# Selecting carries by one key per node, and scanning node terms with their marks in PSUM, in a four-layer graph network

## The chip, the cores and the metric

The kernel runs on one core of one Trainium2 chip. The metric is the device time of one execution in microseconds. The times of three runs and one further, profiled execution are known.

## The reference

There are 6,250 nodes with 96 features and 200,000 edges sorted by destination. Four residual layers follow each other: a graph attention layer with 4 heads (softmax over the edges that enter a node), two rounds of a segment maximum with edge features, two rounds of a segment mean, and three rounds of a degree-normalised segment sum; after each layer the rows are normalised. What matters here is the attention layer:

```python
h = (x @ W).reshape(N, HEADS, HEAD_DIM)
a_src = jnp.einsum('nhd,hd->nh', h, att_src)
a_dst = jnp.einsum('nhd,hd->nh', h, att_dst)
e = jax.nn.leaky_relu(a_src[src] + a_dst[dst], SLOPE)
m = jax.ops.segment_max(e, dst, num_segments=N)
e = jnp.exp(e - m[dst])
denom = jax.ops.segment_sum(e, dst, num_segments=N)
alpha = e / denom[dst]
out = jax.ops.segment_sum(alpha[:, :, None] * h[src], dst, num_segments=N)
```

## The kernel before

**Layout.** The edges, padded to 128 x 1568, lie so that partition p holds the edges p*T to (p+1)*T-1 (T = 1568), in order of destination. A node's edges are therefore neighbours in one partition, or run over from one partition into the next. A segment sum or maximum is a scan along the free dimension, and what a partition hands to the next one is a "carry".

**The passes.** The first three passes (attention, and the two maxima) gather a row per edge: each pass has 196 slots of 8 edges per partition, a slot has 8 indirect DMAs issued by POOL (L449), and the rows go into a ring of 4 buffers. POOL waits for a buffer until its block has been stored (L486); VectorE combines and scans the block, ScalarE writes it back and stores it. After a pass POOL gathers the last row of each node (L506). The other five passes sum by matmuls over a matrix of counts (L723), which is built during the two maxima passes from "step tables" that VectorE makes in pieces between the slots of the attention pass (`table_piece`, L1325).

**The opening, in order.** POOL gathers runs of destinations (L441), and VectorE gets from them the first edge of every node (`startN`, L1347). From then on:

- POOL gathers slot 0 (L456), writes the attention terms of the nodes to the place of their first edge in DRAM (`ad_starts`, 49 scatters, L460 to L463), gathers slot 1, waits for ARENA to be loaded (`ad_loaded`), gathers one more row of node terms (L467), and goes on with slots 2 to 195.
- SP's queue, in order: it stores the starts, loads the ends (L584), stores the last rows of the nodes (L589), broadcasts them into ROWB (L591), waits for `rowb_used`, broadcasts the starts into ROWB (L593), waits for `rowb_used` again and for the 49 scatters (L595), and loads `ad_starts` into ARENA (L596). ROWB is a part of ARENA.
- VectorE makes the last rows (L1361), the marks `same` (1 where an edge has the same destination as the one before, L1368) and the resets (L1375), and then the selection SEL16, a matrix of 128 partitions by 6,272 nodes: it is 1 where the node's last edge lies in the block of partition p+1 and its first edge before that block. This takes three comparisons (L1379, L1380, L1394), the third on the broadcast starts. PE sums each node's column of it (L845), and VectorE takes the result (L1399).
- Then VectorE waits for the row of L467 (`ad_first`), and spreads the node terms along the edges in a scan for each head (AD is ARENA seen as column by head, so that a head's columns are 4 elements apart): the first 112 columns at L1413, the other 1,456 at L1244, one head in each of the slots 0 to 3 of the attention pass. Those columns are first used in slot 14.

**The attention pass.** At slot u VectorE makes the logits of slot u+1 and the states of slot u (L1450, L1458: the scan whose factors ScalarE has put into PSUM), and then does one piece: pieces 0 to 3 are the scans of L1244, 4 to 24 make the step tables, and after 26 come seven groups of an offset. The order is written out at L1465 to L1472:

```python
if u < 2 * TABLE_ITERS:
    table_piece(u)
elif u < 2 * TABLE_ITERS + NG:
    add_offset(u - 2 * TABLE_ITERS)
```

ScalarE stores each chunk of the tables in a slot fixed by the same count (L937 to L944). ScalarE's order in the opening is the node phase, a square root (L989), and then the attention pass, which begins with a wait for `pass_begun` (L920).

PSUM has psO (2,048 columns of float32), psA, psB and psX. psO holds the products of the node phases, in the attention pass the step tables' sums from piece 11 on, and the products of the carries after it.

Of the kernel before, what the change touches and what calls it, by code (L numbers as in the profile page):

```python
# [80 lines left out]
AD_FIRST = 14 * S  # L81
COLUMNS_SLOT = 12


# [14 lines left out]
def build(nc, x, src, dst, dst_before, src_tiles, dst_tiles, edge_attr, att_W, att_src, att_dst, gat_bias, proj_WT, proj_b, ln_g, ln_b,  # L99
# [7 lines left out]
    def sem(name):  # L107
        return ctx.enter_context(nc.semaphore(name))
# [108 lines left out]
    all_edges = sb("all_edges", [1, 1])  # L217
    bound = sb("bound", [P, 2])
    whole = sb("whole", [P, 1])
# [48 lines left out]
    RUNS = EG[:, 0:2 * GB * RUN].bitcast(I32).rearrange("p (s j r) -> p s j r", s=2, j=GB)  # L268
    BELOW = EG[:, 2 * GB * RUN:3 * GB * RUN].rearrange("p (j r) -> p j r", j=GB)
    SHIFT = SEL16[:, 0:4 * P].bitcast(F32).rearrange("p (a m) -> p a m", a=2)  # L270

# [3 lines left out]
    ETERM = psO[:, :].rearrange("p (s b c) -> p s b c", s=2, b=2)  # L275
    psM = [psA, psB, psX]
    step_sums = [psA[:, 0:CW], psB[:, 0:CW], psX[:, 512:512 + CW]]
    STEP_PS = psO[:, :].rearrange("p (a k) -> p a k", a=4)[:, :, 0:CH]
# [33 lines left out]
    ad_loaded = sem("ad_loaded")  # L312
    ad_first = sem("ad_first")
    gathered = [sem(f"gathered{r}") for r in range(RING)]
    tiles_loaded = sem("tiles_loaded")
# [200 lines left out]
    def _(sp):  # L516
# [75 lines left out]
        sp.wait_ge(rowb_used, 1)  # L592
        sp.dma_start(ROWB, start_row[0:NPAD].partition_broadcast(P)).then_inc(rowb_loaded, 16)  # L593
        sp.wait_ge(rowb_used, 2)
        sp.wait_ge(ad_scattered, 16 * NB)  # L595
# [281 lines left out]
    def _(act):  # L877
# [25 lines left out]
        def attention_pass():  # L903
# [19 lines left out]
            for u in range(SLOTS):  # L923
                if u:
                    act.wait_ge(scanned, u)
                act.wait_ge(exp_in, u + 1)
                nc.scalar.activation(EX[:, u % 2, 0, :, :], EX[:, u % 2, 0, :, :], ACT.Exp).then_inc(scales_made, 1)
                nc.scalar.activation(weights, EX[:, u % 2, 1, :, :], ACT.Exp).then_inc(exp_done, 1)
                if u + 2 < SLOTS:
                    head_resets(u + 2)  # L930
                act.wait_ge(scales_made, u + 1)
                nc.scalar.copy(scales[:, :, 1:K9].rearrange("p (h w) k -> p h w k", w=HW),
                               EX[:, u % 2, 0, :, 1:K9].unsqueeze(2).broadcast_to([P, HEADS, HW, S])).then_inc(scales_ready, 1)
                if u:
                    rows_back(u - 1)
                    store(u - 1)
                c = (u - 2 - COLUMNS_SLOT) // 3  # L937
                if (u - 2 - COLUMNS_SLOT) % 3 == 0 and c in range(CHUNKS):
                    act.wait_ge(stage_ready, c + 1)
                    act.dma_start(step_cols[:, :, c * CH:(c + 1) * CH], STAGE[:, c % 2, :, :]  # L940
                                  ).then_inc(stage_stored[c % 2], 16)
                if u == 2 * TABLE_ITERS + 1:
                    act.wait_ge(step_row_ready, 1)
                    act.dma_start(step_rows, ROW_I[:, 0, :]).then_inc(step_row_stored, 16)  # L944
# [73 lines left out]
        node_phase(ATT)  # L1018
        root(dis[:, :])
        attention_pass()  # L1020
        exp(QT[:, 1, :])
# [66 lines left out]
    def _(dve):  # L1088
# [52 lines left out]
        link(nc.vector.tensor_copy(bound[:, 0:1], bound_i[:, :]))  # L1141
        link(ts(bound[:, 1:2], bound[:, 0:1], float(T), None, ALU.add))

# [98 lines left out]
        def ad_along_rest(h):  # L1242

            link(nc.vector.tensor_tensor_scan(out=AD[:, AD_FIRST:T, h], data0=same[:, AD_FIRST:T], data1=AD[:, AD_FIRST:T, h],  # L1244
                                              initial=AD[:, AD_FIRST - 1, h:h + 1], op0=ALU.mult, op1=ALU.add))
# [114 lines left out]
        dve.wait_ge(ends_back, 16)  # L1360
        link(ts(lastf[:, :], ends[:, :], -1.0, 0.0, ALU.add, ALU.max))  # L1361
        dve.sem_inc(rows_out, 1)
        dve.wait_ge(node_idx, 1)
# [14 lines left out]
        dve.wait_ge(rowb_loaded, 16)  # L1378
        link(ts(SEL16, ROWB, bound[:, 0:1], None, ALU.is_ge))  # L1379
        link(stt(SEL16, ROWB, bound[:, 1:2], SEL16, ALU.is_lt, ALU.mult))  # L1380
        dve.sem_inc(rowb_used, 1)
# [10 lines left out]
        link(ts(wneg[:, :], wrow[:, :], -1.0, BIG, ALU.add, ALU.mult))  # L1392
        dve.wait_ge(rowb_loaded, 32)
        link(stt(SEL16, ROWB, bound[:, 0:1], SEL16, ALU.is_lt, ALU.mult))  # L1394
        dve.sem_inc(rowb_used, 1)
        dve.sem_inc(small_ready, 1)
# [12 lines left out]


        dve.wait_ge(ad_first, 16)
        for h in range(HEADS):
            link(nc.vector.tensor_tensor_scan(out=AD[:, 0:AD_FIRST, h], data0=same[:, 0:AD_FIRST], data1=AD[:, 0:AD_FIRST, h],  # L1413
                                              initial=0.0, op0=ALU.mult, op1=ALU.add))
# [6 lines left out]
        def attention_pass():  # L1421
# [43 lines left out]
            for u in range(SLOTS):  # L1465
                if u + 1 < SLOTS:
                    logits(u + 1)
                states(u)
                if u < 2 * TABLE_ITERS:
                    table_piece(u)  # L1470
                elif u < 2 * TABLE_ITERS + NG:
                    add_offset(u - 2 * TABLE_ITERS)  # L1472

# [380 lines left out]
```

## Time and profile before

| what | us |
|---|---|
| median of 3 runs | 8222.67 |
| lowest and highest | 8220.35, 8223.56 |
| the profiled execution, its time | 8213.33 |
| the profiled execution, its span | 8211.5 |

| engine | busy us | share of the span |
|---|---|---|
| PE (matmul) | 4235.5 | 52% |
| VectorE | 5538.0 | 67% |
| ScalarE | 1494.4 | 18% |
| POOL | 4891.3 | 60% |

A busy share is an average over stages. The span has an opening of about 208 us, three passes of gathers up to about 6570 us, and 1641 us of sums by matmul. The chain of waits follows the end of the span back, at each step to what released it; "issue" is time in which an engine waited for nothing that the profile shows. POOL's DMA instructions are rows of its own with a duration; a row in brackets at the end of a line tells how long the engine was idle before it, and what ended that.

### The profile page before, as it was taken

Reading aid. Unit: us, or ns where it says so; the run is one execution under the profiler, and the core shown is the slowest. Engines: PE = TensorE matmul, PEld = TensorE weight load, DVE = VectorE, ACT = ScalarE, POOL = GpSimd, SP = SyncE. Lnnn points to the kernel's source line nnn. Section 1 sums busy time; section 2 is a strip of 40 time slices with the busy share of each in tenths; the row PEclk is TensorE's granted clock in tenths of the full one; section 3 lists DMA queues with packets and bytes.
Section 4 is the critical chain, followed back from the end, with each engine's and each line's share of the span. In section 5 each row is a group of like instructions: output and inputs, shape, how many; then the busy total and the mean of one; then the engine's idle time right before and its main releaser. Section 6 shows DMA issues by size and latency. Waiting matters only on the chain.

```text
span 8211.5 us, 69615 instructions
## 1 busy us (share of the span) xinstructions
PE 4235.5 (52%) x19184; PEld 2465.7 (30%) x19184; DVE 5538.0 (67%) x13229; ACT 1494.4 (18%) x2140; POOL 4891.3 (60%) x5030
## 2 busy tenths in 40 slices
PE   2100000000155655656555555556565498999999
PEld 1000000000131111111113111111111298999999
DVE  4765555555578888888886888888888775222222
ACT  0222222222231121111111111111211200010000
POOL 6777777777637777777776777777777600000000
PEclk6555555555566565565655555565555599999999
DMA  5333333333224444444443444444444275766767
GB/s 145 86 93 86 85 86 85 86 85 86 66 86 130 129 129 132 131 130 130 129 130 103 129 130 132 130 130 129 130 131 131 80 263 201 267 225 227 268 220 247
DMA packets 642303, 1132.83 MB, mean 138 GB/s; under 512 B 164860, under 2 KB 422287, under 8 KB 641634
## 3 DMA queue, kind: packets, MB, share of 16 engines
q1 hardware_dynamic: 360256, 440.38, 16.7%
q0 software_dynamic: 159184, 251.10, 15.5%
q10 hardware_dynamic: 122578, 438.40, 13.4%
q14 instruction: 210, 1.72, 0.1%
q8 instruction: 75, 1.23, 0.1%
HBM read 716.67 MB, written 412.70 MB: 138 GB/s over the span
## 4 chain that ended last, share of the span: by engine, by line
POOL 57%; PE 20%; issue 18%; DVE 3%; ACT 1%; DMA 1%; DVEq 0%; POOLq 0%; ACTq 0%; SPq 0%
POOL CG L449 55%; PE psB L723 6%; PE psX L723 6%; PE psA L723 6%; PE psO L668 1%; POOL ad_starts L461 1%; POOL EG L506 1%; ACT X L1001 1%; POOL EG L441 0%; PE psX L660 0%; PE psO L783 0%; DVE BUF L1120 0%; DVE EG L1172 0%; PE psO L671 0%; DVE halves L1176 0%
## 5 line engine op out<-in xcount | busy, mean ns | idle before, releaser
L449 POOL DMA_INDIRECT CG<-table,BUF x4704 | 4532.5, 964 | 1564.2 <-issue 1432.1
L695 PE MATMUL psO<-WE,BUF 128*128 128x384 f32 x1568 | 1137.3, 880 | 106.8 <-DMA BUF<-in_edge_attr 99.8
L766 PE MATMUL psA<-ident,F 128*100 128x128 f32 x1 | 0.5, 452 | 1740.0 <-DVEq L1404 1740.0
L475 POOL CAST CG<-EG x35 | 26.9, 769 | 1297.9 <-DVEq L1173 1297.9
L953 ACT COPY psX<-BUF 128x384 f32<-128x384 f32 x392 | 189.0, 482 | 3210.7 <-DVE STG L1531 1618.2
L695 PEld LDWEIGHTS psO<-WE,BUF 128*128 128x128 f32 x1568 | 460.6, 324 | 619.4 <-DMA BUF<-in_edge_attr 371.6
L1429 DVE TENSOR_TENSOR terms<-CG,ARENA 128x32 f32<-128x32 f32 x196 | 45.1, 230 | 792.5 <-DMA CG<-table,BUF 792.0
L1493 DVE TENSOR_SCALAR BUF<-iota,EG 128x392 bf16<-128x392 f16 x1568 | 542.3, 346 | 0.0
L766 PEld LDWEIGHTS psA<-ident,F 128*100 128x100 f32 x1 | 0.2, 158 | 1740.3 <-DVEq L1404 1740.3
L702 PE MATMUL psB<-BUF 128*128 128x392 bf16 x523 | 251.2, 480 | 511.4 <-DVE BUF L1499 511.2
L702 PE MATMUL psA<-BUF 128*128 128x392 bf16 x523 | 252.1, 482 | 506.4 <-DVE BUF L1499 506.4
L723 PE MATMUL psA<-CG,BUF 128*128 128x288 bf16 x4018 | 509.9, 287 | 6.2 <-DMA BUF<-counts 6.2
L723 PE MATMUL psB<-CG,BUF 128*128 128x288 bf16 x4018 | 509.2, 287 | 7.1 <-DMA BUF<-counts 7.1
L702 PE MATMUL psX<-BUF 128*128 128x392 bf16 x522 | 251.4, 482 | 504.6 <-DVE BUF L1499 504.6
L1490 DVE TENSOR_SCALAR BUF<-iota,EG 128x128 bf16<-128x128 f16 x1568 | 496.4, 317 | 20.6 <-DMA EG<-step_rows 20.6
L723 PE MATMUL psX<-CG,BUF 128*128 128x288 bf16 x3969 | 500.8, 286 | 0.6 <-POOL CG L478 0.6
L723 PEld LDWEIGHTS psA<-CG,BUF 128*128 128x128 bf16 x4018 | 495.4, 142 | 9.5 <-POOL CG L478 6.7
L723 PEld LDWEIGHTS psB<-CG,BUF 128*128 128x128 bf16 x4018 | 495.1, 142 | 9.8 <-issue 7.5
L1499 DVE TENSOR_SCALAR BUF<-iota,EG 128x392 bf16<-128x392 f16 x1568 | 495.9, 316 | 0.0
L723 PEld LDWEIGHTS psX<-CG,BUF 128*128 128x128 bf16 x3969 | 488.3, 142 | 1.6 <-POOL CG L478 0.8
L1524 DVE TENSOR_TENSOR XTQ<-CG,psO 128x768 f32<-128x768 f32 x196 | 288.6, 1473 | 216.5 <-DMA CG<-table,BUF 216.3
L1524 DVE TENSOR_TENSOR STG<-CG,psO 128x768 f32<-128x768 f32 x196 | 288.8, 1473 | 207.4 <-DMA CG<-table,BUF 206.8
(279 smaller groups left out, 7912.3 us busy)
## 6 DMA issues: line engine op xcount, KB each, us to landing
BUF<-counts SPq DMA_DIRECT2D x245, 784.0 KB, 5.8
BUF<-counts ACTq DMA_DIRECT2D x245, 784.0 KB, 6.2
counts<-BUF SPq DMA_DIRECT2D x1572, 98.0 KB, 2.4
hist<-CG ACTq DMA_DIRECT2D x392, 384.0 KB, 2.5
hist<-CG ACTq DMA_DIRECT2D x196, 416.0 KB, 2.6
CG<-table,BUF POOLq DMA_INDIRECT x4704
BUF<-in_edge_attr SPq DMA_DIRECT2D x392, 128.0 KB
table<-TB SPq DMA_DIRECT2D x14, 336.0 KB, 2.6
```

The costliest lines, as they stand in the source:

```text
L449: pool.indirect_dma_start(out=rows_in[:, u % RING, k, :], out_offset=None, in_=tab, in_offset=bass.IndirectOffsetOnAxis(ap=SRC[:, u * S + ...
L461: pool.indirect_dma_start(out=ad_starts, out_offset=bass.IndirectOffsetOnAxis(ap=start_i[:, b:b + 1], axis=0), in_=ADN[:, b, :], in_offset ...
L506: pool.indirect_dma_start(out=EG[:, b * width:(b + 1) * width], out_offset=None, in_=rec, in_offset=bass.IndirectOffsetOnAxis(ap=last_i[:, ...
L668: mm = pe.matmul(OUTG[:, k, 0:cols], XT[0:depth, g % 2, k * P:(k + 1) * P], WR[0:depth, f, 0:cols], start=True, stop=f != PROJ)
L695: mm = pe.matmul(ETERM[:, s, a, 0:4 * DIM], EA[:, s, a, :], WE[:, m, :, :].rearrange("k c d -> k (c d)"), start=True, stop=True)
L702: pe.matmul(sums, LO[:, j, 0, :], RHS[:, j, 0, :], start=True, stop=False)
L723: mm = pe.matmul(sums[:, 0:3 * DIM], CNT16[:, B % 3, b:b + NB * (P - 1) + 1:NB], PARTS[:, b, :], start=b == 0, stop=b == NB - 1, skip_grou ...
L953: nc.scalar.copy(reset_cols[:, :, 1:K9], reset[:, u * S:(u + 1) * S].unsqueeze(1).broadcast_to([P, DIM // 2, S])).then_inc(resets_ready, 1)
L1490: ts(LO[:, j, 0, :], iota16[:, 0:P], STEP[:, 2, n:n + 1], None, ALU.is_equal)
L1493: ts(RHS[:, j, 0, :], iota16[:, :], STEP[:, 0, n:n + 1], None, ALU.is_equal)
L1499: ts(RHS[:, j, 1, :], iota16[:, :], STEP[:, 1, n:n + 1], None, ALU.is_equal).then_inc(onehot_ready, 1)
L1524: tt(max_cols[b][:, :, 1:K9].rearrange("p c (a k) -> p c a k", a=2), ROWSW[:, r, :, :].rearrange("p (a k) c -> p c a k", a=2), ETERM[:, s, ...
```

## The change

The last row of a node and its first are turned into block numbers (e // T, by a shift, a multiplication and a shift in integers). The node's key is T times the block of its last row, or 0 where both lie in one block. The key is what SP stores and broadcasts, and a single equality with the partition's bound, T*(p+1), gives SEL16. The second broadcast, the second and third comparison, the second wait of SP and the second bound go. ScalarE copies the marks `same` to PSUM (SAME, in psO) after its square root, and the eight scans of node terms read them there, after a wait for that copy. All pieces of the attention pass begin in slot 4 in place of slot 0, with ScalarE's stores of the tables.

```diff
@@ -80,6 +80,9 @@
 COLUMNS_SLOT = 12
+PIECES_FROM = 4
+SPLIT_BITS, SPLIT_MULT, SPLIT_SHIFT = 5, 2675, 17
+assert all(((e >> SPLIT_BITS) * SPLIT_MULT) >> SPLIT_SHIFT == e // T for e in range(EPAD + 1))
@@ -215,7 +218,7 @@
-    bound = sb("bound", [P, 2])
+    bound = sb("bound", [P, 1])
@@ -267,6 +270,7 @@
+    KEY = EG[0:NB, 3600:3600 + 2 * P].bitcast(I32).rearrange("p (a m) -> p a m", a=2)
@@ -274,6 +278,7 @@
+    SAME = psO[:, 0:T]
@@ -311,6 +316,7 @@
+    same_copied = sem("same_copied")
@@ -590,8 +596,6 @@
         sp.dma_start(ROWB, last_row[0:NPAD].partition_broadcast(P)).then_inc(rowb_loaded, 16)
         sp.wait_ge(rowb_used, 1)
-        sp.dma_start(ROWB, start_row[0:NPAD].partition_broadcast(P)).then_inc(rowb_loaded, 16)
-        sp.wait_ge(rowb_used, 2)
         sp.wait_ge(ad_scattered, 16 * NB)
@@ -934,12 +938,13 @@
-                c = (u - 2 - COLUMNS_SLOT) // 3
-                if (u - 2 - COLUMNS_SLOT) % 3 == 0 and c in range(CHUNKS):
+                piece = u - PIECES_FROM
+                c = (piece - 2 - COLUMNS_SLOT) // 3
+                if (piece - 2 - COLUMNS_SLOT) % 3 == 0 and c in range(CHUNKS):
...
-                if u == 2 * TABLE_ITERS + 1:
+                if piece == 2 * TABLE_ITERS + 1:
@@ -1017,6 +1022,7 @@
         root(dis[:, :])
+        nc.scalar.copy(SAME, same).then_inc(same_copied, 1)
         attention_pass()
@@ -1139,7 +1145,6 @@
-        link(ts(bound[:, 1:2], bound[:, 0:1], float(T), None, ALU.add))
@@ -1241,7 +1246,7 @@
-            link(nc.vector.tensor_tensor_scan(out=AD[:, AD_FIRST:T, h], data0=same[:, AD_FIRST:T], data1=AD[:, AD_FIRST:T, h],
+            link(nc.vector.tensor_tensor_scan(out=AD[:, AD_FIRST:T, h], data0=SAME[:, AD_FIRST:T], data1=AD[:, AD_FIRST:T, h],
@@ -1359,6 +1364,13 @@
         link(ts(lastf[:, :], ends[:, :], -1.0, 0.0, ALU.add, ALU.max))
+        link(nc.vector.tensor_copy(KEY[:, 0, :], starts[:, :]))
+        link(nc.vector.tensor_copy(KEY[:, 1, :], lastf[:, :]))
+        link(ts(KEY, KEY, SPLIT_BITS, None, ALU.logical_shift_right))
+        link(ts(KEY, KEY, float(SPLIT_MULT), None, ALU.mult))
+        link(ts(KEY, KEY, SPLIT_SHIFT, None, ALU.logical_shift_right))
+        link(tt(ends[:, :], KEY[:, 0, :], KEY[:, 1, :], ALU.is_lt))
+        link(stt(lastf[:, :], KEY[:, 1, :], float(T), ends[:, :], ALU.mult, ALU.mult))
         dve.sem_inc(rows_out, 1)
@@ -1376,8 +1388,7 @@
         dve.wait_ge(rowb_loaded, 16)
-        link(ts(SEL16, ROWB, bound[:, 0:1], None, ALU.is_ge))
-        link(stt(SEL16, ROWB, bound[:, 1:2], SEL16, ALU.is_lt, ALU.mult))
+        link(ts(SEL16, ROWB, bound[:, 0:1], None, ALU.is_equal))
         dve.sem_inc(rowb_used, 1)
@@ -1390,9 +1401,6 @@
-        dve.wait_ge(rowb_loaded, 32)
-        link(stt(SEL16, ROWB, bound[:, 0:1], SEL16, ALU.is_lt, ALU.mult))
-        dve.sem_inc(rowb_used, 1)
         dve.sem_inc(small_ready, 1)
@@ -1408,9 +1416,10 @@
+        dve.wait_ge(same_copied, 1)
         dve.wait_ge(ad_first, 16)
         for h in range(HEADS):
-            link(nc.vector.tensor_tensor_scan(out=AD[:, 0:AD_FIRST, h], data0=same[:, 0:AD_FIRST], data1=AD[:, 0:AD_FIRST, h],
+            link(nc.vector.tensor_tensor_scan(out=AD[:, 0:AD_FIRST, h], data0=SAME[:, 0:AD_FIRST], data1=AD[:, 0:AD_FIRST, h],
@@ -1466,10 +1475,11 @@
                 states(u)
-                if u < 2 * TABLE_ITERS:
-                    table_piece(u)
-                elif u < 2 * TABLE_ITERS + NG:
-                    add_offset(u - 2 * TABLE_ITERS)
+                piece = u - PIECES_FROM
+                if 0 <= piece < 2 * TABLE_ITERS:
+                    table_piece(piece)
+                elif 0 <= piece < 2 * TABLE_ITERS + NG:
+                    add_offset(piece - 2 * TABLE_ITERS)
```

## Rows read from the trace of the kernel before

**Rows 1.** The page's chain that ended last, by line.

```profile
POOL CG L449 55%; PE psB L723 6%; PE psX L723 6%; PE psA L723 6%; PE psO L668 1%; POOL ad_starts L461 1%; POOL EG L506 1%; ACT X L1001 1%; POOL EG L441 0%; PE psX L660 0%; PE psO L783 0%; DVE BUF L1120 0%; DVE EG L1172 0%; PE psO L671 0%; DVE halves L1176 0%
```

**Rows 2.** Groups by line, POOL: operation, count, busy us, mean ns, idle us and releasers.

```profile
L449 POOL DMA_INDIRECT CG<-table,BUF x4704 | 4532.5, 964 | 1564.2 <-issue 1432.1 <-DMA table<-TB 131.5 <-DVEq L1238 0.3
...
L461 POOL DMA_INDIRECT ad_starts<-ADN,start_i x49 | 64.3, 1312 | 14.9 <-issue 14.9
```

**Rows 3.** Chain in order of time, 190 to 230 us: start, length, what.

```profile
195.10 10.78 DMA ARENA<-ad_starts
...
206.64 0.94 POOL ARENA L467
```

**Rows 4.** Timeline of POOL, 127 to 171 us: start, length, instruction, idle before.

```profile
130.54 1.70 POOL L461 DMA_INDIRECT ad_starts<-ADN,start_i  x1 [0.31 <-issue]
132.55 0.98 POOL L461 DMA_INDIRECT ad_starts<-ADN,start_i  x1 [0.30 <-issue]
...
141.70 4.21 POOL L461 DMA_INDIRECT ad_starts<-ADN,start_i  x1 [0.30 <-issue]
146.21 6.48 POOL L461 DMA_INDIRECT ad_starts<-ADN,start_i  x1 [0.30 <-issue]
...
163.29 7.48 POOL L461 DMA_INDIRECT ad_starts<-ADN,start_i  x1 [0.30 <-issue]
```

**Rows 5.** Timeline of VectorE, 128 to 211 us.

```profile
128.57 0.42 DVE L1361 TENSOR_SCALAR lastf<-ends 49x128 f32<-49x128 f32 x1 [16.32 <-DMA ends<-start_row]
...
129.60 1.79 DVE L1368 TENSOR_TENSOR BUF<-CG 128x1568 f32<-128x1568 int32 x1
...
141.57 3.48 DVE L1379 TENSOR_SCALAR SEL<-ARENA,bound 128x6272 bf16<-128x6272 f32 x1 [6.73 <-DMA ARENA<-last_row]
145.09 6.75 DVE L1380 SCALAR_TENSOR_TENSOR SEL<-ARENA,bound,SEL 128x6272 bf16<-128x6272 f32 x1
...
163.16 6.75 DVE L1394 SCALAR_TENSOR_TENSOR SEL<-ARENA,bound,SEL 128x6272 bf16<-128x6272 f32 x1 [8.62 <-DMA ARENA<-start_row]
171.62 0.21 DVE L1399 TENSOR_SCALAR cpen<-psB 128x49 f32<-128x49 f32 x1 [1.71 <-PE psB L845]
209.03 1.67 DVE L1413 TENSOR_TENSOR_SCAN ARENA<-BUF,ARENA 128x112 f32<-128x112 f32 x4 [37.20 <-DMA ARENA<-ad_nodes,dst]
```

**Rows 6.** Timeline of VectorE, 216 to 255 us.

```profile
216.23 2.03 DVE L1458 TENSOR_TENSOR_SCAN STG<-psX,STG 128x900 f32<-128x900 f32 x1
218.18 3.23 DVE L1244 TENSOR_TENSOR_SCAN ARENA<-BUF,ARENA 128x1456 f32<-128x1456 f32 x1
...
246.24 0.21 DVE L1429 TENSOR_TENSOR terms<-CG,ARENA 128x32 f32<-128x32 f32 x1 [3.69 <-DMA CG<-table,BUF]
...
251.72 3.23 DVE L1244 TENSOR_TENSOR_SCAN ARENA<-BUF,ARENA 128x1456 f32<-128x1456 f32 x1
```

**Rows 7.** Timeline of POOL, 216 to 256 us.

```profile
216.81 0.94 POOL L449 DMA_INDIRECT CG<-table,BUF  x1 [0.30 <-issue]
...
219.30 2.85 POOL L449 DMA_INDIRECT CG<-table,BUF  x1 [0.30 <-issue]
...
227.46 3.30 POOL L449 DMA_INDIRECT CG<-table,BUF  x1 [0.30 <-issue]
...
239.80 3.50 POOL L449 DMA_INDIRECT CG<-table,BUF  x1 [0.30 <-issue]
...
252.39 3.31 POOL L449 DMA_INDIRECT CG<-table,BUF  x1 [0.30 <-issue]
```

**Rows 8.** Timeline of ScalarE, 153 to 214 us.

```profile
153.22 0.24 ACT L989 ACTIVATE dis<-dis 128x49 f32<-128x49 f32 x1 [75.67 <-DVEq L1387]
211.50 0.34 ACT L908 COPY reset_heads<-BUF 128x32 f32<-128x32 f32 x2 [58.04 <-DVEq L1463]
...
213.52 0.82 ACT L932 COPY psX<-EX 128x800 f32<-128x800 f32 x1
```

**Rows 9.** Timeline of VectorE, 39 to 40 us.

```profile
39.78 0.15 DVE L1142 TENSOR_SCALAR bound<-bound 128x1 f32<-128x1 f32 x1
```

## The prediction

> **What bounds the kernel now.** The chain of waits comes first: POOL's row gathers of L449 hold 55% of the span, more than all matmuls together [rows 1]. The groups by line say how tightly: the 4,704 gathers take 964 ns each, and of the 1,564.2 us that POOL idles before them 1,432.1 us is "issue", 0.30 us ahead of each; the rest is three waits for a node table [rows 2]. There is no idle time before a gather that waits for a stored block or for another engine's result. So through the three edge passes POOL sets the pace, and whatever shortens POOL there shortens the kernel one for one. The opening is POOL's too: 49 scatters at L461, 64.3 us with 14.9 us of issue [rows 2], then the load of the node terms into ARENA, then one gather, then the stream of gathers [rows 3].
>
> The mean of a scatter is 1,312 ns [rows 2], the ordinary one 0.98 us. The timeline shows where the rest is: four take 1.70, 4.21, 6.48 and 7.48 us [rows 4]. Laid beside VectorE's timeline, the last three each fall under one long VectorE instruction and end 0.8 to 0.9 us after it: 4.21 under the selection's first comparison (141.57 to 145.05), 6.48 under the second (L1380, to 151.84), 7.48 under the third (L1394, to 169.91) [rows 4, 5]. The broadcast loads of the selection's rows aren't the cause: the first is under way until the comparison that waits for it begins at 141.57, and the scatter at 132.55 still takes 0.98 [rows 4, 5]. The same is seen at the four long scans of L1244, 3.23 us each: the gather that each catches takes 2.85, 3.30, 3.50 and 3.31 us where 0.94 is ordinary [rows 6, 7]. The scan of L1458, 2.03 us, has one operand in PSUM, and the gather at 216.81, wholly under it, takes 0.94 [rows 6, 7]. So what holds POOL is a VectorE instruction that reads two tensors of SBUF (or that runs at two elements per cycle, as L1379 does: 6,272 in 3.48 us), and not one with one operand in PSUM. POOL is held for about the instruction's length, less the part in which POOL did other things.
>
> **The change, part by part, on POOL's path.**
>
> The two comparisons L1380 and L1394 go, each over 6,272 columns with SEL16 and ROWB read from SBUF. The scatters under them give back 6.48 - 0.98 = 5.50 us and 7.48 - 0.98 = 6.50 us: 12.0 us in all. The comparison that stays (is_equal for is_ge, same shape and types) I keep at 3.48 us and its stall at 4.21 - 0.98 = 3.23 us. Its start moves against POOL's beat of 1.29 us, so the stall may be 2.5 to 3.5; were is_equal to run at one element a cycle, with its single SBUF input it would hold POOL as little as L1458 does, and the 3.23 us would go too. Both ends go into the range.
>
> The scatters end 12.0 us sooner, and so must what follows. The ARENA load starts when the last scatter has landed, at 195.10 [rows 3]. Its other condition is the release of ROWB, on SP's queue ahead of it: now the second release, after 169.91, later the only one, after the comparison that ends at 145.05 today [rows 5]. The keys push that by 2 us, to about 147, against 183 for the last scatter: 36 us of cover. So all 12.0 us arrive at the load and at the first gather behind it. SP also loses one broadcast load of 3.1 MB; it lies beside the scatters and is worth nothing.
>
> The keys add seven VectorE instructions on 49 partitions by 128 or 256 elements. The same 49 by 128 takes 0.42 us in L1361 [rows 5], the nearest row; with 0.03 us between them that is at most 3.2 us, and the like of 0.2 us (a small operation, as L1399 [rows 5]) gives 1.6 at least. I take 2.0. They stand before the store of the last rows, so SP's store, the broadcast load and the comparison all come 2 us later; VectorE is next wanted by POOL's path only at 209.03, after 37.20 us of idleness [rows 5] that become some 37.2 - 12.0 - 2.0 + 6.75 + 6.75 + 8.62 (the wait for the second load, gone) = 45 us. That wait hides the keys; with the cover gone, they would cost their 2.0 us. On POOL they may add little stalls, and they shift the comparison of L1368, which today costs 1.70 - 0.98 = 0.72 us and could cost 0 to 1.5. I take +0.3 for all of that, with -0.9 and +1.6 as ends.
>
> The copy of the marks into PSUM is ScalarE's, 1,568 columns. ScalarE copies 800 columns to PSUM in 0.82 us, so some 1.6 us [rows 8], and twice that would change nothing. It starts behind the root at 153.22, where ScalarE is idle for 58.04 us [rows 8]. The added wait for it stands on VectorE ahead of the four short scans and of everything of the pass, but the copy is done near 155 and those scans begin near 197. Zero.
>
> The scans of node terms now have one operand in PSUM. In length I leave them at 3.23 us: 2.22 ns per column, against 2.03/900 = 2.26 for the scan that reads PSUM already [rows 6]. For POOL they become like L1458: 2.85 + 3.30 + 3.50 + 3.31 - 4 x 0.94 = 9.2 us are given back [rows 7]. The trace has no scan with this step of four elements and a PSUM operand, so the saving has the bounds 0 (it still holds POOL) and 9.2; the nearest row is L1458, also a scan, and I take 9.2. The four short scans of L1413, 1.67 us together [rows 5], get the same operand; of 112 columns each, they slip between POOL's accesses already, and I count nothing.
>
> Moving the pieces to the fifth slot is worth about nothing. In the first slots VectorE is behind, and it catches up sooner; but POOL waits for it in neither case [rows 2]. With the scans, a slot of VectorE is 251.72 - 246.24 + 3.23 = 8.7 us [rows 6], and POOL's is 8 x (0.94 + 0.31) = 10.0, so VectorE keeps 1.3 us to spare where it now has 3.69. The terms scanned in slots four to seven are first read in slot 14. ScalarE's stores of the tables and the offsets move along with the pieces, four slots or 40 us, into a pass of 196 slots. The other short stalls of the pieces go with them unchanged. The instruction of L1142 leaves the opening chain: 0.2 us [rows 9].
>
> The sum: -12.0 - 9.2 - 0.2 + 0.3 = **-21.1 us**. On the profiled execution (span 8211.5, time 8213.33) that is 8192.2. The median of the runs is 8222.67, 9.3 us above that execution; the stalls are of fixed length, so I take the same 21.1 us off it: 8201.6, -0.26%.
>
> On such stalls the Trainium skill says (SBUF — State Buffer, the practical consequences of its port section) that an instruction with two SBUF inputs blocks a GpSimd instruction only on its reads, and infers that descriptor generation needs the write interface alone. By that inference neither the comparisons nor the scans would hold a gather, and the sum would be about zero; the 7.48 us scatter under L1394 speaks against it [rows 4].
>
> **The rivals.** (a) The scans keep holding POOL, because of their length or their stepped output in SBUF, of which the trace has no case with PSUM. For it: only that absence. Against: L1458 and the gathers under it. Then -12.0 alone counts: 8222.67 - 12.0 = 8210.7. Chance 0.08.
>
> (b) VectorE's two-operand instructions don't hold POOL; the long scatters and gathers have another cause that only coincides with them, so the comparisons go and the scans change, and the stalls stay. 8222.7 (plus or minus 1). Against it: each long entry starts under a long VectorE instruction and ends within 0.9 us of its end [rows 4 to 7]. Chance 0.03. The skill's inference above would end here.
>
> (c) Slower. The scans with their stepped SBUF operand and a PSUM operand run far slower than either row, and VectorE becomes the bound in slots four to seven. The first 1.3 us more per scan are free, then the ring of four buffers lends about one slot (10 us, an estimate: a block is stored about 20 us after its gather, its buffer wanted after 30). With x us more per scan the loss is 4(x - 1.3) - 10. It eats the 21.1 us at x = 9.1, that is at scans of 12.3 us, 8.5 ns per column against 2.26 measured. At six times today's length (x = 16.2) it is 8222.7 + 49.6 - 21.1 = 8251. Chance 0.01.
>
> (d) Unforeseen shifts of phase between POOL and VectorE over the three passes, either way by several us; the gathers' mean of 964 against 944 ns is 94 us of such stalls in all [rows 2]. A twentieth of it more or less is 5 us. Chance that this takes the result out of the forecast's own range: 0.04, half of it towards no gain.
>
> **How the numbers follow.** The forecast has 0.84. Its own range: down by 3.2 (the remaining comparison not holding POOL) and 0.9, up by 1.6 and by some 3 of phase and of run scatter (the three runs lie within 3.2 us): 8197 to 8206. To reach rival (a), at 8210.7, the range goes up to 8211: with (a) it holds 0.92 of the cases on paper, and less allowing for what I have not seen. About 0.2%, or 16.4 us, is what a measurement of this kernel can tell from no change. The forecast with its range is beyond it (8206.2 is the border): faster 0.83. Rivals (a) and (b) and half of (d) are within: same 0.14. Slower, (c) and the unforeseen: 0.03.
>
> **What the profile after would show.** No scatter over 5 us, just one of about 4.2 under the equality; scatters' total down from 64.3 to about 52 us; the ARENA load starting near 183 and the first gather behind it near 196; the four scans in slots four to seven at 3.2 to 3.3 us, with the gathers beside them at 0.94; VectorE's idle time ahead of the first scan longer, not shorter. I am wrong if those gathers still take 3.3 us (a), if a scatter of 6 us remains (b), if POOL idles before a gather for a stored block (c), or if all of this is seen and the pass still ends less than 18 us sooner (d).

## The result and the profile after

The changed kernel takes 8200.35 us (median of 9 runs, 8191.73 to 8204.42), the kernel before 8221.36 beside it (9 runs, 8220.16 to 8226.31). The difference is 21.0 us; the ratio is 0.9971 with a 95% interval of 0.9963 to 0.9979. The forecast was 8201.6, 21.1 us below. (A few executions of either kernel in the groups below took hundreds or thousands of microseconds longer; the ratios leave them out.) The profiled execution of the changed kernel took 8202.16 us, its span 8200.2. That is only 11.3 us shorter than the span of before, and why it is so is a finding of its own (last section).

The groups by line of POOL, after (the answer to [rows 2]):

```profile
L455 POOL DMA_INDIRECT CG<-table,BUF x4704 | 4532.3, 963 | 1567.5 <-issue 1432.6 <-DMA table<-TB 134.3 <-DVEq L1243 0.3
...
L467 POOL DMA_INDIRECT ad_starts<-ADN,start_i x49 | 52.0, 1060 | 14.9 <-issue 14.9
```

The scatters took 64.3 us and take 52.0. The waits ahead of the gathers are of the same kinds as before: 1432.6 us of issue, 134.3 us for the three node tables, 0.3 us for VectorE, and none for a stored block. (The row of before has the 0.3 us too; the prediction took it as nothing.)

POOL's timeline from 135 to 147 us, the answer to [rows 4]:

```profile
135.03 1.43 POOL L467 DMA_INDIRECT ad_starts<-ADN,start_i  x1 [0.30 <-issue]
...
145.93 4.04 POOL L467 DMA_INDIRECT ad_starts<-ADN,start_i  x1 [0.30 <-issue]
```

These are the only two scatters above 1.2 us. Where four were long, there is the one that runs into the comparison of destinations (1.43) and the one that runs into the equality (4.04). The timeline of VectorE from 130 to 255 us answers to [rows 5, 6]:

```profile
130.99 0.22 DVE L1367 CAST EG<-starts 49x128 int32<-49x128 f32 x1
...
132.93 0.28 DVE L1373 SCALAR_TENSOR_TENSOR lastf<-EG,ends 49x128 f32<-49x128 int32 x1
...
146.36 3.48 DVE L1391 TENSOR_SCALAR SEL<-ARENA,bound 128x6272 bf16<-128x6272 f32 x1 [7.31 <-DMA ARENA<-last_row]
...
197.25 1.67 DVE L1422 TENSOR_TENSOR_SCAN ARENA<-psO,ARENA 128x112 f32<-128x112 f32 x4 [42.72 <-DMA ARENA<-ad_nodes,dst]
...
242.97 3.23 DVE L1249 TENSOR_TENSOR_SCAN ARENA<-psO,ARENA 128x1456 f32<-128x1456 f32 x1
247.47 0.21 DVE L1438 TENSOR_TENSOR terms<-CG,ARENA 128x32 f32<-128x32 f32 x1 [1.27 <-DMA CG<-table,BUF]
```

The seven instructions of the keys take 2.2 us (130.99 to 133.21). The equality takes 3.48 as the comparison did, the scan with its marks in PSUM 3.23 as the one without. VectorE idles 42.72 us ahead of the short scans, so all that was added there is covered.

POOL's timeline from 194 to 257 us, the answer to [rows 3, 7]: the gather behind the load, and gathers beside two of the long scans.

```profile
194.85 0.95 POOL L473 DMA_INDIRECT ARENA<-ad_nodes,dst  x1 [2.54 <-DMA ARENA<-ad_starts]
...
243.64 0.95 POOL L455 DMA_INDIRECT CG<-table,BUF  x1 [0.31 <-issue]
244.89 0.95 POOL L455 DMA_INDIRECT CG<-table,BUF  x1 [0.30 <-issue]
...
253.65 0.94 POOL L455 DMA_INDIRECT CG<-table,BUF  x1 [0.31 <-issue]
```

The gather at 243.64 lies wholly under the scan of 242.97 to 246.20 and takes 0.95 us; before, such a one took 3.3. The row at 206.64 of before has come to 194.85, 11.8 us sooner. ScalarE's copy to PSUM, in its timeline near 151 us:

```profile
151.53 1.46 ACT L1025 COPY psO<-BUF 128x1568 f32<-128x1568 f32 x1
```

### The profile page after: what moved, and what is told of

Read it like the earlier page. It is cut to its first block, busy times and chain, and to the rows that moved or that the text cites. A ratio compares the mean times of both kernels' runs of the same rounds, so it can differ in the third digit from the quotient of the medians.

```text
span 8200.2 us, 69617 instructions
## 1 busy us (share of the span) xinstructions
PE 4244.0 (52%) x19184; PEld 2467.5 (30%) x19184; DVE 5524.8 (67%) x13233; ACT 1496.4 (18%) x2141; POOL 4879.7 (60%) x5030
## 4 chain that ended last, share of the span: by engine, by line
POOL 57%; PE 20%; issue 19%; DVE 3%; ACT 1%; DMA 1%; DVEq 0%; POOLq 0%; ACTq 0%; SPq 0%
POOL CG L455 55%; PE psX L727 6%; PE psB L727 6%; PE psA L727 6%; PE psO L672 1%; POOL EG L447 1%; POOL EG L512 1%; POOL ad_starts L467 1%; ACT X L1006 1%; PE psX L664 0%; DVE EG L1177 0%; PE psO L787 0%; DVE BUF L1126 0%; PE psO L675 0%; DVE halves L1181 0%
## 5 line engine op out<-in xcount | busy, mean ns | idle before, releaser
L455 POOL DMA_INDIRECT CG<-table,BUF x4704 | 4532.3, 963 | 1567.5 <-issue 1432.6
## 6 DMA issues: line engine op xcount, KB each, us to landing
BUF<-in_edge_attr SPq DMA_DIRECT2D x392, 128.0 KB
```

What stands on the lines that cost most here:

```text
L455: pool.indirect_dma_start(out=rows_in[:, u % RING, k, :], out_offset=None, in_=tab, in_offset=bass.IndirectOffsetOnAxis(ap=SRC[:, u * S + ...
```

## The experiments

Four groups of runs, each with runs of the kernel before on its own chip, and a probe that was executed once, in group 3 (8205.33 us, read for its rows alone). The median of before is 8221.36, 8214.86, 8223.48 and 8211.74 us in the four, so only distances within a group are compared.

| kernel | group | us, median | to before, us | ratio, 95% interval |
|---|---|---|---|---|
| changed | 1 | 8200.35 | -21.0 | 0.9971 (0.9963 to 0.9979) |
| changed, again | 2 | 8189.31 | -25.5 | 0.9971 (0.9958 to 0.9983) |
| scans from SBUF | 2 | 8197.78 | -17.1 | 0.9980 (0.9971 to 0.9989) |
| key alone | 2 | 8199.98 | -14.9 | 0.9982 (0.9973 to 0.9991) |
| scans alone | 2 | 8203.17 | -11.7 | 0.9987 (0.9978 to 0.9997) |
| equality in 16 | 3 | 8196.72 | -26.8 | 0.9970 (0.9958 to 0.9981) |
| all cut short | 3 | 8187.79 | -35.7 | 0.9959 (0.9945 to 0.9973) |
| changed, beside | 3 | 8198.82 | -24.7 | 0.9971 (0.9960 to 0.9981) |
| all cut short, again | 4 | 8176.60 | -35.1 | 0.9954 (0.9940 to 0.9967) |
| changed, third | 4 | 8190.90 | -20.8 | 0.9975 (0.9966 to 0.9984) |

### The changed kernel again

No edit.

> The changed kernel once more, to see what varies by itself. Theory: in the opening and in slots 4 to 7 the same rows as in its first profile (first gather behind the load near 196, no gather over 1.0 us beside the four scans), but an ordinary gather's period that may be anything from 1.248 to 1.251 us, and a time that follows it: 4,704 gathers x 2.4 ns = 11 us between a profile with the one and with the other. Rival: the longer period (1.2509 us against 1.2484 before) is a price of the change itself; then it is seen here again, and never in the kernel before.

Measured: the ordinary gather takes 944 ns here, as in the kernel before, where the first profile of the same changed kernel had 947. The longer period is no price of the change; it comes and goes between executions of one kernel (rows in the last section). The span is 8187.5 us, and the same stretch of the opening is as short as in the first profile.

### Scans from SBUF

```diff
-            ... data0=SAME[:, AD_FIRST:T] ...
+            ... data0=same[:, AD_FIRST:T] ...
-        nc.scalar.copy(SAME, same).then_inc(same_copied, 1)
-        dve.wait_ge(same_copied, 1)
```

and the same for the four short scans.

> The changed kernel, but the eight scans read their marks from SBUF again, and the copy to PSUM is gone; the pieces still begin in the fifth slot. Theory (the second SBUF operand holds POOL): the four gathers beside the long scans take 2.85 to 3.5 us again, 9.2 us in all, and the time is 9 us above the changed kernel: about 8209.5. Rival (the gain of the scans came from their later slot, where VectorE no longer lags): those gathers stay at 0.95 us, and the time is that of the changed kernel, 8200.

Measured: 8.5 us above the changed kernel of its group (8197.78 to 8189.31). Both engines' timelines from 241 to 283 us; the other two scans look the same:

```profile
241.41 3.23 DVE L1248 TENSOR_TENSOR_SCAN ARENA<-BUF,ARENA 128x1456 f32<-128x1456 f32 x1
242.08 3.31 POOL L455 DMA_INDIRECT CG<-table,BUF  x1 [0.30 <-issue]
...
278.52 3.23 DVE L1248 TENSOR_TENSOR_SCAN ARENA<-BUF,ARENA 128x1456 f32<-128x1456 f32 x1
279.19 3.31 POOL L455 DMA_INDIRECT CG<-table,BUF  x1 [0.30 <-issue]
```

In slots 4 to 7 a scan with both operands in SBUF costs POOL 3.31 - 0.94 = 2.37 us, 9.5 in all. The operand does it; the later slot doesn't end the holding. (The 8209.5 of the expectation was counted from group 1; within the group 9 us were expected and 8.5 measured.)

### The key alone

The kernel above with `PIECES_FROM = 0`: of the change, only the key, the equality and the loads and comparisons that went.

> The kernel before with the key and the single equality alone: scans from SBUF, pieces from the first slot. Theory (two comparisons of 6.75 us held POOL for 5.50 and 6.50 us): 12 us below the kernel before, about 8209.5, no scatter over 5 us, and the same as the kernel with scans from SBUF in the fifth slot to within 2 us, since the slot is worth nothing. Rival (the later slot is worth something): 3 us or more above that kernel.

Measured: 14.9 us below before where 12 were expected, 2.2 above the kernel with the scans in the fifth slot. The long gathers beside the scans take 2.85, 3.31, 3.31 and 3.31 us: 9.0 us over the ordinary, against 9.5 in the later slots. The slot is worth nothing by the rows, and 2.2 us of medians (2 were expected at most) is within what executions differ. The scatters are down to 52.5 us.

### The scans alone

The keys' seven instructions go, the second bound comes back, and:

```diff
-        link(ts(SEL16, ROWB, bound[:, 0:1], None, ALU.is_equal))
+        link(ts(SEL16, ROWB, bound[:, 0:1], None, ALU.is_ge))
+        link(stt(SEL16, ROWB, bound[:, 1:2], SEL16, ALU.is_lt, ALU.mult))
+        sp.dma_start(ROWB, start_row[0:NPAD].partition_broadcast(P)).then_inc(rowb_loaded, 16)
+        sp.wait_ge(rowb_used, 2)
+        link(stt(SEL16, ROWB, bound[:, 0:1], SEL16, ALU.is_lt, ALU.mult))
```

> The changed kernel with the three comparisons, the second broadcast load and its wait put back, and the keys taken out: only the scans' part of the change. Theory: 9 us below the kernel before, about 8212, the scatters of 6.5 and 7.5 us back, total of the scatters near 64 us. Were the two parts to share a gain (one hidden by the other), this and the key alone would add up to more or less than the 21.0 us of both together; by the theory they add up.

Measured: 11.7 us below before where 9 were expected. Both engines' timelines from 142 to 173 us:

```profile
142.56 3.96 POOL L467 DMA_INDIRECT ad_starts<-ADN,start_i  x1 [0.30 <-issue]
...
146.42 6.75 DVE L1388 SCALAR_TENSOR_TENSOR SEL<-ARENA,bound,SEL 128x6272 bf16<-128x6272 f32 x1
146.82 7.21 POOL L467 DMA_INDIRECT ad_starts<-ADN,start_i  x1 [0.30 <-issue]
...
164.49 6.75 DVE L1402 SCALAR_TENSOR_TENSOR SEL<-ARENA,bound,SEL 128x6272 bf16<-128x6272 f32 x1 [8.60 <-DMA ARENA<-start_row]
164.63 7.46 POOL L467 DMA_INDIRECT ad_starts<-ADN,start_i  x1 [0.30 <-issue]
```

With the comparisons the two long scatters are back at once; the scatters' total is 65.0 us. The second broadcast load is back too, but it isn't what holds POOL: of the eight scatters from 154.33 us on, most of them in the 8.60 us in which VectorE waits for it, none takes more than 0.99 us.

By the medians of one group the two parts add up: 14.9 + 11.7 = 26.6 us alone, 25.5 together. The rows give less. The last gather of the first pass starts at 2155.07 us with the key alone and at 2159.54 with the scans alone, against 2166.51 before: 11.4 and 7.0 us, 18.4 in sum, where both together have 20.1 (below). So neither part hides the other, but the 3 us by which each median exceeds its expectation are not explained by the edit.

### The probe

```diff
+        for _ in range(3):
+            link(tt(PC, PA, PB, ALU.add))
+        for _ in range(3):
+            link(tt(PC, SAME, PB, ALU.add))
+        for _ in range(2):
+            link(ts(PC, PA, 1.0, None, ALU.mult))
+        for _ in range(2):
+            link(ts(PC, SAME, 1.0, None, ALU.mult))
+        for _ in range(2):
+            link(stt(PC, PA, 1.0, PB, ALU.mult, ALU.add))
         dve.wait_ge(ad_first, 16)
```

PA, PB and PC are unused parts of SBUF of 1,568 columns; two of them are filled with zeros first.

> The changed kernel with a row of VectorE instructions of 1,568 float32 columns each, put under the later scatters, where VectorE has nothing to do (behind the column sums of the selection, ahead of the wait for the node terms): three additions of two SBUF tensors, three of one PSUM and one SBUF tensor, two scalings SBUF to SBUF, two scalings PSUM to SBUF, two multiply-and-adds of two SBUF tensors. They compute nothing that is used. Theory (two SBUF inputs, or the fast mode, hold POOL): each scatter that falls under an addition or multiply-and-add of two SBUF tensors takes 0.5 to 1.7 us more than 0.98, and under a fast scaling (about 1 us) 0.1 to 0.9 more; under the forms with PSUM every scatter takes 0.98, the additions being as long as the others. Rival (length alone holds POOL, or any use of SBUF): the forms with PSUM cost the same as those without. Rival from the page's inference (a tensor_tensor takes only the read interface): the additions of two SBUF tensors cost nothing either, and only the scalings do.

VectorE's timeline from 154 to 175 us, equal instructions merged:

```profile
154.45 5.45 DVE L1424 TENSOR_TENSOR BUF<-BUF 128x1568 f32<-128x1568 f32 x3
159.93 5.44 DVE L1426 TENSOR_TENSOR BUF<-psO,BUF 128x1568 f32<-128x1568 f32 x3
165.41 1.99 DVE L1428 TENSOR_SCALAR BUF<-BUF 128x1568 f32<-128x1568 f32 x2
167.43 3.62 DVE L1430 TENSOR_SCALAR BUF<-psO 128x1568 f32<-128x1568 f32 x2
171.08 3.69 DVE L1432 SCALAR_TENSOR_TENSOR BUF<-BUF 128x1568 f32<-128x1568 f32 x2
```

POOL's timeline over the same stretch:

```profile
154.36 0.98 POOL L467 DMA_INDIRECT ad_starts<-ADN,start_i  x1 [0.30 <-issue]
155.64 1.45 POOL L467 DMA_INDIRECT ad_starts<-ADN,start_i  x1 [0.30 <-issue]
157.40 1.52 POOL L467 DMA_INDIRECT ad_starts<-ADN,start_i  x1 [0.31 <-issue]
159.23 1.52 POOL L467 DMA_INDIRECT ad_starts<-ADN,start_i  x1 [0.30 <-issue]
161.05 0.98 POOL L467 DMA_INDIRECT ad_starts<-ADN,start_i  x1 [0.30 <-issue]
162.34 0.98 POOL L467 DMA_INDIRECT ad_starts<-ADN,start_i  x1 [0.30 <-issue]
163.62 0.98 POOL L467 DMA_INDIRECT ad_starts<-ADN,start_i  x1 [0.30 <-issue]
164.91 1.59 POOL L467 DMA_INDIRECT ad_starts<-ADN,start_i  x1 [0.30 <-issue]
166.81 1.44 POOL L467 DMA_INDIRECT ad_starts<-ADN,start_i  x1 [0.31 <-issue]
168.55 0.98 POOL L467 DMA_INDIRECT ad_starts<-ADN,start_i  x1 [0.30 <-issue]
169.84 0.98 POOL L467 DMA_INDIRECT ad_starts<-ADN,start_i  x1 [0.30 <-issue]
171.12 0.98 POOL L467 DMA_INDIRECT ad_starts<-ADN,start_i  x1 [0.30 <-issue]
172.41 1.40 POOL L467 DMA_INDIRECT ad_starts<-ADN,start_i  x1 [0.30 <-issue]
174.11 1.52 POOL L467 DMA_INDIRECT ad_starts<-ADN,start_i  x1 [0.30 <-issue]
```

Three additions of 1.8 us with both operands in SBUF: scatters of 1.45, 1.52 and 1.52 us. Three of the same length with one operand in PSUM: 0.98 each. The fast scalings of 1.0 us: 1.59 and 1.44; those from PSUM, 1.8 us long: 0.98. The two multiply-and-adds: 0.98 for the scatter that starts 0.04 us behind the first, then 1.40 and 1.52. The forms with both in SBUF hold POOL and their like with PSUM don't, so neither length nor writing to SBUF is the cause. The expectation gave 0.5 to 1.7 us for an addition; it is 0.47 to 0.54, the low edge. The rows show why it is so little. A held scatter ends 0.82 to 0.86 us after the addition that holds it; after 0.30 us of issue the next one starts, some 1.1 us into the next addition, and waits only for the 0.7 us that are left. So POOL falls into the beat of the additions, one scatter in 1.82 us where it would take 1.28. A single long instruction costs it much more: 6.50 of 6.75 us.

The rows also show that the two kinds of instruction hold at different points. One with two SBUF inputs holds only a scatter that starts under it: the one at 154.36 is under way when the first addition begins 0.09 us later, and takes 0.98. In this profile and the first of the changed kernel, up to 560 us, no comparison, addition or scan of two SBUF tensors of 0.9 us or more lengthens an entry that it finds under way. A fast form does: the equality begins 0.43 us into the scatter at 145.93, the first fast scaling 0.50 us into the one at 164.91, and these end 0.13 and 0.1 us after the instruction, not 0.82 or more. (Not always: in the first profile of the changed kernel two fast forms of 1,792 columns take 1.28 us themselves, where three others take 1.07, and leave the entry that they meet at 0.94 and 0.95.)

The inference of the Trainium skill (SBUF — State Buffer, practical consequences) that a two-input addition leaves descriptor generation alone does not hold here for indirect DMAs: it costs 0.47 to 0.54 us a scatter. The prediction counted an indirect DMA as no read of SBUF. The rule that stands beside it in the same section, that an instruction with two SBUF inputs contends with a GpSimd instruction that reads SBUF, would give the holding if an indirect DMA reads its indices from SBUF at its start. The rows name the indices as an input (`start_i`), and only entries that start under such an instruction are held; no run here takes the indices away to test it. What the same section states of the fast forms, that they contend with GpSimd, agrees with the 0.46 and 0.61.

### The equality in 16

```diff
-        link(ts(SEL16, ROWB, bound[:, 0:1], None, ALU.is_equal))
+        for c0 in range(0, NPAD, 392):
+            link(ts(SEL16[:, c0:c0 + 392], ROWB[:, c0:c0 + 392], bound[:, 0:1], None, ALU.is_equal))
```

> The changed kernel with its one equality over 6,272 columns cut into 16 of 392. Theory (POOL is held for one instruction's length and gets in between two): no scatter over 1.3 us, the 4.1 us entry gone, the opening 2.5 to 3.1 us shorter, the time 3 us below the changed kernel, which the scatter between executions may hide. Rival (16 short ones hold POOL as long in sum as one long one): the same 3 us spread over three or four scatters, nothing won.

Measured: 2.1 us below the changed kernel of its group, where 3 were expected; the medians can't tell it from nothing, the rows can. Both engines' timelines from 146 to 149 us:

```profile
146.09 8.04 DVE L1392 TENSOR_SCALAR SEL<-ARENA,bound 128x392 bf16<-128x392 f32 x16 [6.63 <-DMA ARENA<-last_row]
146.31 1.05 POOL L467 DMA_INDIRECT ad_starts<-ADN,start_i  x1 [0.30 <-issue]
147.67 0.98 POOL L467 DMA_INDIRECT ad_starts<-ADN,start_i  x1 [0.30 <-issue]
```

The 4-us scatter is gone and the scatters take 48.8 us, 3.2 less than in the first profile of the changed kernel. The price is VectorE's: 16 short ones take 8.04 us where one took 3.48. That is idle time of VectorE here.

### All cut short

```diff
-            link(tt(BELOW, RUNS[:, g % 2, :, :], node_f[:, here]..., ALU.is_lt))
+            for j in range(GB):
+                link(tt(BELOW[:, j:j + 1, :], RUNS[:, g % 2, j:j + 1, :], ..., ALU.is_lt))
-        link(tt(same[:, :], DST, PREV, ALU.is_equal))
+        for o in range(0, T, 224):
+            link(tt(same[:, o:o + 224], DST[:, o:o + 224], PREV[:, o:o + 224], ALU.is_equal))
```

and in the same way the tile codes and tile parts (in 448 and 256 columns), the rows of steps (in 392 and 224), and the equality as above.

> The kernel meant to beat both: the changed one with every long VectorE instruction that holds POOL in the opening and in the table pieces cut into pieces of 224 to 448 columns (the comparison of runs, the marks, the equality, the tile codes and parts, the rows of steps). The changed kernel's first profile shows 6.97 us over the ordinary under the seven comparisons of runs, 0.48 + 3.10 at the marks and the equality, and 13.0 us in the pieces of the pass. Theory: most of these 23 us go, less what the short ones still cost: 14 to 22 us below the changed kernel. Rival (VectorE's longer pieces, up to 6.5 us in a slot that leaves it 4.3, make POOL wait): gathers in slots 26 to 30 idle for a stored block, and the gain of the pieces is lost there.

> The changed kernel once more, beside the two kernels that are to be compared with it on this chip. Theory: 21 us below the kernel before, plus or minus 3; ordinary gathers at 1.248 or at 1.251 us from one execution to the next.

Measured: 35.7 us below before, 11.0 below the changed kernel of its group. That misses the 14 to 22 expected. Waits of POOL from 40 to 110 us, in this kernel:

```profile
POOL EG L447 <- issue: 13.7, 45, 0.3
POOL CG L455 <- DMA table<-TB: 4.1, 1, 4.1
POOL EG L447 <- DVEq L1240: 2.1, 1, 2.1
```

and in the changed kernel's second profile:

```profile
POOL EG L447 <- issue: 14.0, 46, 0.3
POOL CG L455 <- DMA table<-TB: 1.7, 1, 1.7
```

Over the first 560 us the entries above 1.0 us hold 22.7 us beyond the ordinary in the changed kernel beside it and 5.9 in this one: 16.8 us of holding are gone. But 2.1 + 4.1 - 1.7 = 4.5 us are given back in the opening: the comparison of runs in seven parts takes VectorE 2.95 us in place of 1.79, seven times over, and POOL waits for it once, and at the end for the first table. That is the size of the rival, in another place than it was expected: no gather of slots 26 to 30 waits for a stored block, and one of slot 33 waits 0.4 us. The changed kernel beside it came out 24.7 us below before, just outside the expected 21 plus or minus 3.

### Both once more

> The kernel with all holding instructions cut short once more: five runs left its distance from the changed kernel (11 us in the medians, with executions at two levels 11 us apart) too uncertain. Theory: in the profiles the time over the ordinary in the first 560 us was 22.7 us in the changed kernel and 5.9 in this one, so about 16 us below the changed kernel in like executions, 13 to 19 in the medians. Rival (cutting costs elsewhere what it gives here): 11 us or less.

> The changed kernel beside it, for the comparison. Theory: its profile shows an ordinary gather's period at one of the two levels seen so far, 1.2484 or 1.2509 us, and nothing between them; 21 us below the kernel before, plus or minus 3.

Measured: 14.3 us below the changed kernel, 35.1 below before; the changed kernel itself 20.8 below before. The last gather of the first pass, in four profiles with the same ordinary gather of 944 ns. With everything cut short (two profiles of the same kernel, then in the changed kernel's second and third):

```profile
2132.07 0.94 POOL L455 DMA_INDIRECT CG<-table,BUF  x1 [0.30 <-issue]
```

```profile
2132.89 0.94 POOL L455 DMA_INDIRECT CG<-table,BUF  x1 [0.30 <-issue]
```

```profile
2146.39 0.94 POOL L455 DMA_INDIRECT CG<-table,BUF  x1 [0.30 <-issue]
```

```profile
2145.73 0.94 POOL L455 DMA_INDIRECT CG<-table,BUF  x1 [0.30 <-issue]
```

So 13.6 us in the mean, near the 16.8 - 4.5 = 12.3 of the waits. The kernel with all long instructions cut short beats both, by 35 us against before and by 11 to 14 against the changed one; the 16 us expected for like executions were too many by what the opening gave back, while the 14.3 of the medians lie in the expected 13 to 19.

## Why the prediction was right

**The bound.** POOL set the pace in the opening and the pass, and what was taken from its holding came out at the end of the pass. The last gather of the first pass, at 2166.51 us in the kernel before, is at 2146.39 and 2145.73 in the two profiles of the changed kernel with a like ordinary gather: 20.1 and 20.8 us, against 21.1 forecast. This, and not the median, is what bears the sum out. That the medians of the first group are 21.0 us apart is in part luck: the four groups give 21.0, 25.5, 24.7 and 20.8, and the two like profiles are 24.0 and 24.2 us shorter than before over the whole span. The 3 to 4 us beyond the first pass lie where nothing was changed, and stay unexplained.

**The comparisons, -12.0.** The scatters lost 64.3 - 52.0 = 12.3 us, and 11.8 us arrived at the gather behind the load (0.3 of the 12.3 is the scatter at the comparison of destinations, 1.43 for 1.70). The equality kept its length and holds POOL for 4.04 - 0.98 = 3.06 us (3.23 taken). The cover held, at 33 us for the 36 forecast: the equality ends at 149.84, the load begins at 183.39 (183 forecast). That the comparisons and not the loads did it was an argument from the times at which entries end; the scatters of 0.98 us beside the second load, in the kernel with the comparisons put back, and the probe show it for the two forms.

**The keys, +0.3.** 2.2 us on VectorE (2.0 taken), and nothing above 1.0 us on POOL beside them. The comparison of destinations held POOL 0.45 us in that profile and 1.03 in the next, inside the 0 to 1.5.

**The scans, -9.2.** By the operand in PSUM: no gather beside the four scans is held, and 9.5 us of holding come back with the operand in SBUF in the same slots. From the first gather behind the load to the end of the pass the two like profiles are 8.3 and 8.4 us shorter than before, a little under the 9.2. The bound at 0 and rival (a) fall. With a PSUM operand the step of four elements in the SBUF operand and the output doesn't hold POOL.

**The slot, 0.** VectorE keeps 1.27 us to spare in a slot with a scan (1.3 forecast).

**The copy, 0.** 1.46 us (1.6 taken), done 44 us before it is wanted. The 0.2 us for the bound's instruction was not measured by itself.

**Rivals.** (b), no holding by two-operand forms, falls with the probe. (c), scans far slower, falls with 3.23 us. (d), phases: the waits of the gathers for the three node tables come to between 128.0 and 135.9 us in the profiles, so shifts of several microseconds exist. They didn't take the first group out of the range, but they may be part of why the groups give 20.8 to 25.5 us; that wasn't separated. The 9.3 us between the profiled execution of before and its median, which the prediction left unexplained, are about what a change of the gather's level gives (below); the level of an execution that wasn't profiled isn't known, so this is not shown.

## What to carry to other kernels

Where POOL issues indirect DMAs one after the other and sets the pace, look at the mean of an issue against the ordinary one, and lay the long ones beside VectorE's timeline. A VectorE instruction that reads two SBUF tensors, or a fast one of one tensor, that meets such a DMA costs POOL up to nearly its length (6.50 of 6.75 us here, but 0.54 for each of several additions of 1.8 us in a row); put one operand in PSUM where there is room, drop it where one comparison will do, or cut it to a few hundred columns. Cut only where VectorE has time to spare: the short ones are longer in sum, each by a fixed part (last section), and where POOL waits for VectorE that is given back.

## What was not expected of the hardware

**The ordinary gather has two lengths.** It is 944 ns in nine profiles and 947 in three, with nothing between; the period of the ordinary ones in the first pass is 1.2483 to 1.2487 us, or 1.2509. The answer for the line of the gathers, 1000 to 1500 us (count, shortest, median and longest in ns, first and last start), in the changed kernel's first profile and then in its second:

```profile
L455 POOL DMA_INDIRECT CG<-table,BUF x400: 941/947/1003, 1000.0 to 1499.3; - x134
```

```profile
L455 POOL DMA_INDIRECT CG<-table,BUF x402: 940/944/972, 999.1 to 1499.8; - x134
```

The level belongs to an execution and not to a kernel: the one source of the changed kernel has 947, 944, 947 and 944 in its four profiles. Over 4,704 gathers 2.5 ns are 12 us, more than half of what the change gives. The first profile after (947) is only 11.3 us shorter than the one before (944), while the medians are 21.0 apart; the second (944) is 24.0 us shorter. What sets the level stays open.

**A fast instruction cut in 16 is over twice as long, and POOL has little part in it.** The 16 pieces of 392 columns take 0.50 us each, gaps included, where a sixteenth of the single equality is 3.48/16 = 0.22. The answer for their line gives the shortest, the median and the longest in ns:

```profile
L1392 DVE TENSOR_SCALAR SEL<-ARENA,bound x16: 423/425/648, 146.1 to 153.7; 128x392 bf16<-128x392 f32 x16
```

At least half of them lie within 2 ns of each other, so what lengthens them is a fixed part and not a wait for POOL, which would vary. From 6,272 columns in 3,485 ns and 392 in 423, a column takes 0.52 ns and the fixed part is 0.22 us. (A form of the tables' steps that was cut, 966 ns for 1,568 columns and 351 for 392, also gives 0.52 ns a column, with 0.15 us fixed.) Of the 4.6 us that the cutting costs VectorE, 15 more fixed parts are 3.3, the gaps between the instructions 0.5, and the pieces above 425 ns some 0.7; only these last can be waits for POOL.
